# Trainium2 kernel study: the first batch's W_down loads on ScalarE's queue, b_down behind them

## What is computed

```
h = gelu(x @ W_down[role] + b_down[role])
y = x + h @ W_up[role] + b_up[role]
out = (y - mean(y)) * rsqrt(var(y) + 1e-5) * gamma[role] + beta[role]
```

## Time and profile before

| what | value |
|---|---|
| median of three executions | 365.76 us (365.07 to 366.26) |
| the profiled execution, its own time | 365.14 us |
| its span, first to last instruction | 363.3 us |
| mean granted TensorE clock | 0.995 |
| PE busy | 353.4 us, 97% of the span |
| DVE busy | 288.5 us, 79% |
| ACT busy | 185.5 us, 51% |
| moved by DMA | 96.59 MB, 266 GB/s over the span |

### The profile page before, as it was taken

One profiled execution on the slowest core, in us unless ns is written; L12 is line 12 of the kernel. 1 busy time (PEld: TensorE's weight loads), 2 busy tenths in 40 slices (PEclk: granted clock), 3 DMA queues, 4 the chain that ended last, 5 costly groups with the idle time before them and its releaser, 6 DMA issues.

```text
span 363.3 us, 4947 instructions
## 1 busy us (share of the span) xinstructions
PE 353.4 (97%) x1548; PEld 289.5 (80%) x1548; DVE 288.5 (79%) x296; ACT 185.5 (51%) x295; POOL 40.5 (11%) x73
## 2 busy tenths in 40 slices
PE   6999999999999999999999999999999999999992
PEld 2888888878888888888888888888888888888881
DVE  2897989897896878968798787986789777873476
ACT  4793566762646626564375623656346571615131
POOL 0000221003200112002110021100301002200012
PEclk9999999999999999999999999999999999999997
DMA  7999999989777887789757896696958911570023
GB/s 206 405 390 412 410 411 399 316 298 380 281 258 290 251 327 256 237 302 327 299 196 236 299 357 262 235 362 184 391 166 267 359 58 66 222 258 32 0 115 116
DMA packets 27227, 96.59 MB, mean 266 GB/s; under 512 B 3154, under 2 KB 3410, under 8 KB 27218
## 3 DMA queue, kind: packets, MB, share of 16 engines
q1 hardware_dynamic: 23040, 81.80, 63.2%
q10 hardware_dynamic: 4178, 14.69, 10.2%
HBM read 79.70 MB, written 16.78 MB: 266 GB/s over the span
## 4 chain that ended last, share of the span: by engine, by line
PE 96%; DMA 2%; DVE 1%; SPq 0%; issue 0%; ACT 0%; DVEq 0%
PE up_ps L275 48%; PE down_ps L268 48%; DMA wd_stage<-W_down 1%; DVE h_full L573 0%; DMA roles_sb<-roles 0%; DVE rows L579 0%; DVE up_ps L556 0%; SPq L149 0%; ACT wd_hi L461 0%; SPq L238 0%; DVEq L42 0%; DVE last_mean L566 0%; DVE neg_shift L564 0%; SPq L239 0%; DVEq L555 0%
## 5 line engine op out<-in xcount | busy, mean ns | idle before, releaser
L268 PE MATMUL down_ps<-x_hi,wd_hi 128*128 128x512 f32 x256 | 81.8, 390 | 1.7 <-ACT wd_hi L459 0.9
L268 PE MATMUL down_ps<-x_hi,wd_lo 128*128 128x512 f32 x256 | 81.4, 389 | 0.0
L268 PE MATMUL down_ps<-x_lo,wd_hi 128*128 128x512 f32 x256 | 81.4, 389 | 0.0
L275 PE MATMUL up_ps<-wu_hi,h_hi 128*128 128x512 f32 x256 | 79.6, 389 | 0.1
L275 PE MATMUL up_ps<-wu_hi,h_lo 128*128 128x512 f32 x256 | 79.5, 389 | 0.0
L275 PE MATMUL up_ps<-wu_lo,h_hi 128*128 128x512 f32 x256 | 79.4, 389 | 0.0
L268 PEld LDWEIGHTS down_ps<-x_hi,wd_hi 128*128 128x128 f32 x256 | 47.9, 188 | 12.5 <-issue 2.6
L275 PEld LDWEIGHTS up_ps<-wu_hi,h_hi 128*128 128x128 f32 x256 | 47.9, 188 | 10.5 <-issue 0.5
L275 PEld LDWEIGHTS up_ps<-wu_lo,h_hi 128*128 128x128 f32 x256 | 48.1, 188 | 10.0
L268 PEld LDWEIGHTS down_ps<-x_lo,wd_hi 128*128 128x128 f32 x256 | 48.0, 188 | 10.0
L275 PEld LDWEIGHTS up_ps<-wu_hi,h_lo 128*128 128x128 f32 x256 | 48.0, 188 | 10.0
(11 more groups left out here) (46 smaller groups left out, 253.3 us busy)
## 6 DMA issues: line engine op xcount, KB each, us to landing
wu_stage<-W_up SPq DMA_DIRECT2D x32, 512.0 KB, 7.3
rows<-x SPq DMA_DIRECT2D x32, 512.0 KB, 4.1
x_stage<-xT SPq DMA_DIRECT2D x31, 512.0 KB, 8.4
wd_stage<-W_down SPq DMA_DIRECT2D x31, 512.0 KB, 8.8
out<-rows ACTq DMA_DIRECT2D x28, 512.0 KB, 4.7
b_up_row<-b_up SPq DMA_DIRECT2D x8, 512.0 KB, 3.6
gamma_row<-gamma SPq DMA_DIRECT2D x8, 512.0 KB, 6.4
beta_row<-beta SPq DMA_DIRECT2D x8, 512.0 KB, 7.3
```

What stands on the lines that cost most here:

```text
L268: return pe.matmul(down_ps[:, kc, :], wd_part[:, n, c * K + kc * P:c * K + (kc + 1) * P], x_part[:, n, c * S:(c + 1) * S], start=start, st ...
L275: mm = pe.matmul(up_ps[:, t % 2, half], h_part[:, kc, t * P:(t + 1) * P], wu_part[:, kc, half], start=(kc == 0 and h_part is h_hi and wu_p ...
```

## The change

All loads of the first batch's `W_down` move from SyncE's queue to ScalarE's. SyncE issues x0 to x3 in a row and then waits for the roles; the W_up loads come next on it. ScalarE reads the role itself, behind its unused Gelu, issues wd0a, wd0b and wd1 ahead of its x0 roundings, wd2 behind these, and wd3 and `b_down` behind the roundings of wd0. Its wait for the roles ahead of `first_steps` goes, since it now stands earlier. TensorE's, VectorE's and GpSimd's programs are the same. The kernel after the change has its lines shifted: L149 becomes L152, L345 becomes L342, and so on.

```diff
         @block.sync
...
             sp.dma_start(x_stage[:, 0, S:CPL * S], x_src(0)[:, 0, S:CPL * S]).then_inc(x_landed[0], 16)
+            for i in range(1, NLOAD):
+                load_x_part(0, i)
             sp.wait_ge(roles_landed, 16)
             first_role = load_role(sp, 0)
-            sp.dma_start(wd_stage[:, 0, 0:K], wd_src(first_role)[:, 0, 0:K]).then_inc(first_wd_landed, 16)
-            sp.dma_start(wd_stage[:, 0, K:CPL * K], wd_src(first_role)[:, 0, K:CPL * K]).then_inc(wd_landed[0], 16)
-            for i in range(1, NLOAD):
-                load_x_part(0, i)
-                load_wd_part(first_role, i)
             for i in range(KC):
                 load_wu_part(first_role, i)
...
         @block.scalar
...
+            def load_first_wd_part(i):
+                act.dma_start(wd_stage[:, i, :], wd_src(first_role)[:, i, :]).then_inc(wd_landed[i], 16)
+
             act.dma_start(roles_sb[:, :], roles).then_inc(roles_landed, 16)
-            act.dma_start(b_down_all[:, :], b_down_cols).then_inc(b_down_landed, 16)
+
             act.wait_ge(constants_ready, 2)
             act.activation(unused[:, :], eps[:, :], ACT.Gelu)
+            act.wait_ge(roles_landed, 16)
+            first_role = load_role(act, 0)
+            act.dma_start(wd_stage[:, 0, 0:K], wd_src(first_role)[:, 0, 0:K]).then_inc(first_wd_landed, 16)
+            act.dma_start(wd_stage[:, 0, K:CPL * K], wd_src(first_role)[:, 0, K:CPL * K]).then_inc(wd_landed[0], 16)
+            load_first_wd_part(1)
             act.wait_ge(first_x_landed, 16)
             act.copy(x_hi[:, 0, 0:S], x_stage[:, 0, 0:S]).then_inc(first_x_hi, 1)
             act.wait_ge(x_landed[0], 16)
             act.copy(x_hi[:, 0, S:CPL * S], x_stage[:, 0, S:CPL * S]).then_inc(x_hi_ready, 1)
+            load_first_wd_part(2)
             act.wait_ge(first_wd_landed, 16)
             act.copy(wd_hi[:, 0, 0:K], wd_stage[:, 0, 0:K]).then_inc(first_wd_hi, 1)
             act.wait_ge(wd_landed[0], 16)
             act.copy(wd_hi[:, 0, K:CPL * K], wd_stage[:, 0, K:CPL * K]).then_inc(wd_hi_ready, 1)
+            load_first_wd_part(3)
+            act.dma_start(b_down_all[:, :], b_down_cols).then_inc(b_down_landed, 16)
             for i in range(1, NLOAD):
                 round_x_part(0, i)
                 round_wd_part(0, i)
-            act.wait_ge(roles_landed, 16)
             act.wait_ge(b_down_landed, 16)
             first_steps()
```

More of the change, by code:

```diff
@@ L146, in bass_role_adapter_layernorm, with wd_src @@
         normed = sem("normed")
+        def wd_src(role):
+            return W_down[role].rearrange("(p n c) k -> p n (c k)", n=NLOAD, c=CPL)
         def load_role(eng, batch):
@@ L170, in x_src @@
                 return xT[batch].rearrange("(p n c) s -> p n (c s)", n=NLOAD, c=CPL)
-            def wd_src(role):
-                return W_down[role].rearrange("(p n c) k -> p n (c k)", n=NLOAD, c=CPL)
             def load_x_part(batch, i):
```

## The result

The changed kernel takes **370.99 us** (median of five executions, 369.96 to 371.46) against 365.76 us before (the median of five as well, 365.07 to 369.44); the ratio is 1.0137, 95% interval 1.0104 to 1.0170. Measured again beside other kernels it took 371.29 and 371.15 us, at ratios of 1.0143 (1.0099 to 1.0187) and 1.0145 (1.0114 to 1.0176). The forecast was 371.2. The change costs 5 us of 366.

A forecast was written before the change was run, and what follows sets the result against it. TensorE was taken to bound the kernel, its end set by wd0b's landing at about 7.7 us. A 5.9 us shift on 365.14 or 365.76 gave 371.0 or 371.7; forecast 371.2 us, range 367.0 to 373.2.

The forecast's parts named there:

- What bounds: Whole kernel: TensorE holds 96%; the end is set by wd0b's landing at about 7.7 us.
- When wd0a is issued: Start, ScalarE's queue: wd0a goes out 0 to 0.7 us later than on SyncE, taken as 0.4.
- What is ahead of wd0: Start, transfers: x already queued, up to 2.7 parts, passes ahead of wd0, then both queues share evenly.
- The sum: Start: landing delays plus half-clock matmuls shift TensorE's work by 4.6 to 7.2 us, taken as 5.9.
- the low end: Start: x1 and x2 pass first, x3 shares; wd0a behind about 4 parts, wd0b behind 5; shift 5.9 us, clock down.
- the clock: TensorE's start: over 5 us idle after warm-up halves its clock; the first eight matmuls take 3.4 us.
- The signs: Profile after: wd0b's rounding at 11.5 to 13.5, q10 still before 5 us, x1 to x3 before wd0, PE idle over 4.
- What was put at nothing: Elsewhere: x0 roundings, wd1 to wd3, b_down and second-batch loads move without making TensorE wait; no added time.
- Alternation from the start: Rival at the start: queues alternate packets at once; shift 2.1 to 3.1 us, 367.3 to 368.9 us; chance 0.19.
- The faster rival: Start: two queues move early bytes faster, wd0b lands at 6.6 to 7.1; 364.7 to 365.2 us; chance 0.07.
- rival 4: Start: wd1 or wd3 also late, or more than x passes; shift 7.5 to 9 us, 373 to 375; chance 0.04.
- rival 3: Start: quicker early transfers pay for the parts passing first; no change, 365.8 us within 1.1; chance 0.12.

The follow-up runs named there:

- e1: Kernel before, all loads still on SyncE's queue, but x1 to x3 issued ahead of the wait for the roles and so ahead of wd0; 371.16 us, ratio 1.0142.
- e6: Kernel after, with SyncE waiting for wd0a's landing before it issues x1 to x3 and W_up; 368.04 us, ratio 1.0053.
- e12: Kernel after, unchanged, run again as the partner of a version with a longer warm-up; 371.15 us, ratio 1.0145.
- e8: Kernel after, unchanged, run once more to see how much a start varies; 371.29 us, 5.8 over the kernel before.
- e2: Kernel after, with x1 to x3 issued after SyncE's read of the role, beside wd0a and wd0b; 371.01 us, ratio 1.0136.
- e5: Kernel before, one queue, with SyncE waiting for wd0a's landing before it issues x1 and all that follows; 365.66 us, ratio 0.9984.
- e10: Kernel before, with b_down's load alone moved behind the roundings of wd0; 365.17 us, ratio 0.9990.
- e7: Kernel after, with x1 alone issued ahead of wd0, x2 and x3 held until wd0a has landed; 368.27 us, ratio 1.0066.

## Why the prediction was right

**What bounds.** Right for the start: wd0's landing moved by 4.5 us and everything behind it moved. Incomplete elsewhere. I wrote that TensorE waits "for nothing else but the warm-up's zeros". It loses 0.4 us at 77 us to a split of h, which its list of waits leaves out. That stall returned 0.4 us of the 5.20.

**When wd0a is issued.** The bounds were 0 to 0.7 us late. It was 0.05 us early, at 2.84: ScalarE's queue reads the role while its table load runs (the read starts at 1.9 us, the table load goes from 1.31 to 2.59).

**What is ahead of wd0.** Right, and confirmed from three sides. The kernel after's q10 moved nothing up to 6.5 us; the order alone costs the same on one queue (e1); with x held back the second queue costs wd0 nothing (e6). My step said that x passes because it is queued earlier and that then the two share evenly. The second half needs its unit: they share evenly in packets, 106 to 102, and by 0.41 to 0.19 in MB.

**The sum.** wd0a's rounding was put at 11.5 and came at 10.29, 11.25 and 11.45 in three executions; wd0b's at 12.6 and came at 12.23, 13.21 and 13.36. The forecast itself was the low end's shift of 5.9 us, in which wd0b has 12.37 + 0.77 - 8.50 = 4.6 and the clock 5.9 - 4.6 = 1.3. Measured in the same terms, wd0b's delay, the clock, and the 0.4 us given back:

| profile | its time | wd0b later | clock | given back | sum | span over 363.3 |
|---|---|---|---|---|---|---|
| the kernel after | 369.96 | 4.50 | 0.70 | 0.4 | 4.8 | 4.8 |
| e12 | 371.05 | 5.63 | 0.66 | 0.4 | 5.9 | 5.9 |
| e8 | 372.11 | 5.48 | 1.88 | 0.4 | 7.0 | 7.0 |

e12's is the one nearest to a median execution. There wd0b was 1.0 us later than in my sum, the clock cost half of my 1.3, and a stall that I had not seen gave 0.4 back. The terms are the right ones; that their errors cancel, and that the forecast lies 0.2 us from the median, is luck. One step of the working was wrong besides: I took the 219 GB/s of 5.6 to 7.7 us as a property of the early stage. It isn't. From 4 to 7.5 us the kernel after moves 353 GB/s, and e1, with one queue, has full rate in its row from 7 to 8, where x passes, and a low one from 9 to 10, where wd0's halves do (why, no run shows):

```profile
7.00:8.00 1.00, 0.00 (x0) 0.00 (x0) 0.30 (x1) 0.00 (x0) 0.00 (x0) 1.00 0.98 391
9.00:10.00 1.00, 0.00 (x0) 0.00 (x0) 0.00 (x0) 0.00 (x0) 0.00 (x0) 1.00 0.95 260
```

**The signs.** wd0b's rounding from 11.5 to 13.5, q10 still before 5 us and TensorE idle for over 4 us came as written, and the granted clock was 0.50 under the first real matmuls. That x1 to x3 would land before wd0 held for wd0b, but x3 landed together with wd0a.

**What was put at nothing.** wd1 to wd3, b_down and the second batch's loads cost nothing: TensorE's list of waits has one entry for data. b_down landed at 21.2, where I had written 21, and the W_up roundings began at 21.84, behind it and ScalarE's read of the next role; nothing of TensorE's waited for them.

**The rivals.** Alternation from the start (2.1 to 3.1 us) did not happen in the kernel after. e2 made it happen, and it cost 5.6 us: the rival's mechanism was real and its price less than half of the measured one. In e2's profile wd0b's rounding is 4.4 us late, where the rival had a shift of 2.1 to 3.1 us, and the clock, which it had up, costs another 1.1 (6.54 - 5.40). The first of the two errors is at least in part the landing: the rival counts a transfer as landed when its share of the bytes has passed, and wd0a landed when its queue had moved 0.46 MB instead of 0.26. The Trainium skill's page "DMA: Bandwidth & Descriptors" (Rules for kernel authors) was right that spreading loads over issuing engines brings no bandwidth: from 11 to 14 us two queues move 417 GB/s in the kernel after, where one has 406 from 10 to 18 before. The alternation by packets that it describes (Queues, rings and completion order) agrees with the rows from 7.5 to 9 us, 106 packets to 102; the first 3.7 us, in which only the earlier queue moves, do not follow from it, and there the measurement decides. The faster rival needed more bytes per microsecond from two queues together. There were more in the profile after, 353 GB/s from 4 to 7.5 us against 237, but they were x1's to x3's. No further load became late (rival 4), and nothing offset the parts that passed (rival 3).

## What to carry to other kernels

Ask of every load that is issued earlier or on another queue what it passes: the same DMA engines serve both, so the transfer that the busiest engine waits for should have nothing that is needed later ahead of it, nor beside it on another queue; behind it in the same queue such loads cost nothing here (e5). A change that makes the start late is dearer than its wait if TensorE idles long enough for its granted clock to fall; the time from the last late operand to a later fixed matmul separates the two. And a start that is made earlier can be given back at the next place with little slack, so look for uneven spacing of the matmuls as well as for named waits.

## What was not expected of the hardware

- Two queues together were slower in the early stage than one: 198 GB/s at a DMA share of 0.76 from 4 to 7.5 us (e2), against 353 GB/s at 0.99 with one queue full (the profile after) and 237 at 0.90 (before). It was made up by 10 us. The cause stays open.
- A load issued on an idle queue while the other was full moved nothing for 3.7 us in the kernel after; in e6 x1's rounding began 8.3 us after its issue, with the roles of the queues exchanged. The runs show when this happens and not why.
- The clock, once down, stayed down for different stretches behind the same program: wd0b's rounding to part 1 took 6.10, 6.06 and 7.28 us in three executions, 5.40 at the full clock.
- A transfer of 256 KB can land over a microsecond late by itself: wd0b's rounding at 9.15 instead of 7.73 in e10's profile, in a program whose median time is that of before. The granted clock fell after TensorE's wait of 1.9 us for it, while the wait of 0.88 us before 6.52 in the kernel before did not bring it down.
- A transfer's landing can come well after its share of the bytes: wd0a's 0.26 MB landed when ScalarE's queue had moved 0.46 MB in e2 and 0.94 MB in e7.
